# In the second cross attention, the fills of a slot's first run move in front of the turn of the running maximum

## The chip, the core and the metric

The kernel runs on one core of a Trainium2 chip. Its engines work side by side, each through its own list of instructions in order, and meet at semaphores: PE (TensorE, matmuls and transposes into the PSUM memory), DVE (VectorE), ACT (ScalarE), POOL (GpSimd) and SP, which only issues transfers. The metric is the device time of one execution in microseconds (us), as the median of several runs. The trace is one further execution, recorded instruction by instruction.

## The reference

Two decoder layers over x (4 x 512 x 256) with a context of 4 x 1601 x 256, all in fp32. Each layer is a self attention, a cross attention and a mixture of experts, each followed by a residual and a layer norm. The change touches only the cross attention of the second layer. Cut to what matters:

```
x = layernorm(context, gamma_media, beta_media)      # 1601 rows
latents = layernorm(latents, gamma_lat, beta_lat)    # 512 rows, from the layer before
kv  = concatenate((x, latents * kv_gate))            # 2113 keys
q   = latents @ Wq;  k = kv @ Wk;  v = kv @ Wv       # 8 heads of 64
sim = (q * SCALE) @ k.T                              # fp32
sim = sim - max(sim over all 2113 keys)
attn = softmax(where(valid, sim, -1e30))
out = (attn @ v) @ Wout
```

The maximum over all keys of a query is subtracted before the exponential. So no exponential of a query can be made until the scores of all its keys are there.

## The kernel before

`layer1_cross` (line 1963) cuts the work into 32 units. A unit is one of 4 batches, one of 4 pairs of heads and one half of 256 queries. Its 2113 keys lie in 17 tiles of 128, grouped into 5 runs of 4, 4, 3, 3 and 3 tiles. One step of the outer loop is called a slot here. In slot s, PE makes the scores of unit s, while DVE and ACT lower and exponentiate those of unit s-1, and PE weighs the values with the probabilities of unit s-2. Within a slot the inner loop goes over the five runs (`gi` 0 to 4). Each engine's list is written out by hand in this order; there is no scheduler.

For one slot, the names are these:

- `scores` (L2677): two matmuls a tile of keys. ACT takes the result out of PSUM and adds the mask (L2341), tile by tile; DVE keeps the running maximum over the tiles, in a PSUM bank (L2443 copies the first tile, L2445 takes the maximum with the following ones) and writes the last step into SBUF as `most`, which the trace shows as `l_w` (L2449).
- `turned` (L2688): at the head of the next slot PE transposes `most` in four matmuls, so that DVE can reduce over the partitions (`high`, L2455, gives `nm`). `turned` waits until the last tile's maximum is there.
- `spread_out` (L2695): PE spreads that maximum over a bank, after the first run's scores. DVE subtracts it from the scores from the second run on (`lower`, L2463). ACT makes the exponentials (L2318), POOL sums them (L2232 and following).
- `weigh` (L2654): PE's product of probabilities and values. In the first run it also waits for DVE to have taken the product before (`weighted`, L2471 and L2474, giving `x_o`).
- `fill`: PE makes one more input: K (keys, L2599), V (values, L2606), q (queries, L2588), N (turned context or latents, L2581), O (the output product, L2614), x and L (the next stage's routing). All share one PSUM bank, RB, one after the other. A fill waits until the fill before it has been copied away, by ACT for K, V, q, N and x.

The fills of a run are in two lists. `lead` has the first one if it is of kind q, K or V, and is made at the very head of the run. `trail` has the rest. In the first run of a slot, `trail` holds: a V fill of 4 tiles (8 matmuls) in every even slot from 2 to 30, 15 in all, behind a K fill as lead; an N fill of four transposes in slots 5, 13 and 21, behind a q fill as lead; nothing in other slots. In the slots before the first unit there is no `turned` yet.

ACT's own list for a first run is: the last exponential of unit s-2, the copies of `trail`, then the score copies. DVE's is: `high`, statistics of the next batch's context rows (L2391; at most two in the slots named above), then the running maximum over the first four tiles.

Of the kernel before, what the change touches and what calls it, by code (L numbers as in the profile page):

```python
# [1962 lines left out]
def layer1_cross(nc, top, g):  # L1963
# [20 lines left out]
    with ctx:  # L1984
# [61 lines left out]
        def unit(u):  # L2046

            return u // UB, u % UB // 2, u % 2

        def exists(u):  # L2050
            return 0 <= u < UNITS
# [6 lines left out]
        def uses(s, gi):  # L2058


            made = []
            if s == -1:
                if gi == 0:
                    for i in range(len(CGROUPS) - 1):
                        made += turns(0, i)
                    made += [("K", 0, 0, c) for c in range(PURE)] + turns(0, len(CGROUPS) - 1)
                    made += [("q", 0, 0)] + [("K", 0, 0, c) for c in range(PURE, NG)]
                return made
            b, i = s // UB, s % UB
            p = i // 2  # L2070
            if exists(s):
                if i % 2 == 0:
                    made += [("K", b, p, NG - 1)] if gi == 0 and s > 0 else []
                    made.append(("V", b, p, gi))
                else:
                    nb, np_ = (b, p + 1) if p + 1 < PAIRS_X else (b + 1, 0)
                    if nb < B:
                        made.append(("K", nb, np_, gi - 1) if gi >= 1 else ("q", nb, np_))
                if b + 1 < B and (i, gi) in TURNS:
                    made.append(("N", b + 1) + divmod(TURNS.index((i, gi)), KD))  # L2080
            if b >= 1:
                if i == 2 and gi in (2, 4):
                    made.append(("O", b - 1, gi // 2 - 1))
                if (i, gi) in ((4, 1), (4, 3)):
                    made.append(("x" if gi == 1 else "L", b - 1, 0))
                if (i, gi) in ((7, 1), (7, 3)):
                    made.append(("x" if gi == 1 else "L", b - 1, 1))
            return made

        def lead(s, gi):  # L2090

            return [use for use in uses(s, gi)[:1] if s >= 0 and use[0] in "qKV"]

        def trail(s, gi):
            return uses(s, gi)[len(lead(s, gi)):]
# [23 lines left out]
        def released(eng, use):  # L2119

            if use[0] in BY_ACT:
                eng.wait_ge(moved, MOVED[use])
            else:
                eng.wait_ge(read, READ[use])
# [10 lines left out]
        def piece_of(t):  # L2135
            return next(k for k, (lo, hi) in enumerate(PIECES) if lo <= t < hi)

        def scores_at(u, t):

            k = piece_of(t)  # L2140
            first = 2 * ((u * NPC + k) % 2)
            at = t - PIECES[k][0]
            return first, slice(at * QN, (at + 1) * QN)

        def moved_before(m):

            return m // NPC * KT + PIECES[m % NPC][1]
# [226 lines left out]
        def _(dve):  # L2374
# [10 lines left out]
            def stats(b, i):  # L2385
                src, _, np_ = source(b, i)
                if i == 0:
                    dve.wait_ge(cx_loaded, 48 * b)
                    if b >= 1:
                        dve.wait_ge(shift_ready, STATS_DONE[b - 1, 1 if b >= 2 else 0])  # L2390
                return token(nc.vector.bn_stats(bn[0:np_, i, :], src))  # L2391
# [168 lines left out]
        def _(pe):  # L2560
# [70 lines left out]
            def last_product(half, pairs):  # L2631
                for i in range(2):
                    j = 2 * half + i
                    for p in pairs:
                        mm = nc.tensor.matmul(PS[:, FINAL_OUT[half], i * D:(i + 1) * D], o[:, p, j * P:(j + 1) * P], wo[:, p, :],
                                              start=(i == 0 and p == 0), stop=(i == 1 and p == PAIRS_X - 1))
                if pairs[-1] == PAIRS_X - 1:
                    mm.then_inc(last_out, 1)

            pe.wait_ge(consts, 2)  # L2640
            for s in SLOTS:
                if s == 0:
                    pe.wait_ge(w_loaded, 16 * 3)
                for gi in range(NG):

                    def weigh(u):
                        b, p, hq = unit(u)
                        pe.wait_ge(exp_done, u * NG + gi + 1)
                        if gi == 0 and u >= 1:
                            pe.wait_ge(o_ready, u)  # L2650
                        released(pe, ("V", b, p, gi))
                        for t in TILES[gi]:
                            for h in range(2):
                                mm = nc.tensor.matmul(PS[h * HDX:(h + 1) * HDX, AVB, 0:QN],  # L2654
                                                      vs[:, p % 2, t, h * HDX:(h + 1) * HDX],
                                                      pt[:, u % 2, t, h * QN:(h + 1) * QN],
                                                      start=(t == 0), stop=False)
                        if gi == NG - 1:
                            pe.wait_ge(summed, (u + 1) * SUMS)
                            for h in range(2):  # L2660
                                mm = nc.tensor.matmul(PS[h * HDX:(h + 1) * HDX, AVB, QN:2 * QN], ones[:, 0:HDX],
                                                      total[:, h * QN:(h + 1) * QN], start=False, stop=True)
                        mm.then_inc(av_done, 1)

                    def scores():
                        b, p, hq = unit(s)
                        released(pe, ("K", b, p, gi))
                        released(pe, ("q", b, p))
                        for t in TILES[gi]:
                            k = piece_of(t)  # L2670
                            m = s * NPC + k
                            if t == PIECES[k][0] and m >= 2:
                                pe.wait_ge(s_moved, moved_before(m - 2))
                            first, half = scores_at(s, t)
                            for h in range(2):
                                at = slice(h * HDX, (h + 1) * HDX)
                                mm = nc.tensor.matmul(PS[:, first + h, half], ks[at, t * P:(t + 1) * P],  # L2677
                                                      qs[at, p % 2, hq * QN:(hq + 1) * QN], start=True, stop=True)
                            if t == PIECES[k][1] - 1:
                                mm.then_inc(s_done, 1)  # L2680

                    def turned(u):

                        pe.wait_ge(s_most, u * KT + KT)
                        if u >= 1:
                            pe.wait_ge(lowered, u * NPC)
                        for j in range(SPAN // P):
                            mm = nc.tensor.transpose(PS[:, MB, j * P:(j + 1) * P], most[:, j * P:(j + 1) * P], ident[:])  # L2688
                        mm.then_inc(t_done, 1)

                    def spread_out(u):

                        pe.wait_ge(nm_ready, u + 1)
                        for j in range(SPAN // P):
                            mm = nc.tensor.transpose(PS[:, MB, j * P:(j + 1) * P],  # L2695
                                                     nm[:, u % 2, j:j + 1].to_broadcast([P, P]), ident[:])
                        mm.then_inc(m_done, 1)

                    for use in lead(s, gi):
                        fill(use)  # L2700
                    if s == UNITS and gi == 0:
                        released(pe, BY_NUMBER[-1])
                        last_product(0, (0, 1, 2))
                        pe.wait_ge(s_moved, UNITS * KT)
                        last_product(1, (0, 1))
                    if exists(s - 2):
                        weigh(s - 2)
                    if gi == 0 and exists(s - 1):
                        turned(s - 1)
                    for use in trail(s, gi):  # L2710
                        fill(use)
                    if exists(s):
                        scores()
                    if gi == 0 and exists(s - 1):
                        spread_out(s - 1)
# [212 lines left out]
```

## Time and profile before

| what | value |
|---|---|
| median of 3 runs | 2210.22 us (2209.06 to 2211.64) |
| profiled execution | 2216.79 us, of which the span of the trace is 2214.6 us |
| PE, matmuls | 1984.1 us busy, 90% of the span |
| DVE | 1534.0 us, 69% |
| ACT | 1153.4 us, 52% |
| POOL | 963.9 us, 44% |
| second cross attention with its lead-in | about 880 to 1870 us of the span |

The page's shares are means over stages with different limits. The second cross attention is the stretch from the first score matmul at 909.9 us to the last exponential at 1849.7 us, with the opening and closing steps around it. For this change only this stretch matters, and in it the few microseconds around each `turned`, of which there are 32, one at the start of each slot from 1 to 32. From one `turned` to the next it is 26 to 36 us. In rows of the trace, matmul counts are twice those of the kernel text where the operands are fp32 products (16 for 8), while a transpose counts once.

### The profile page before, as it was taken

Reading aid. Unit: us, or ns where it says so; the run is one execution under the profiler, and the core shown is the slowest. Engines: PE = TensorE matmul, PEld = TensorE weight load, DVE = VectorE, ACT = ScalarE, POOL = GpSimd, SP = SyncE. Lnnn points to the kernel's source line nnn. Section 1 sums busy time; section 2 is a strip of 40 time slices with the busy share of each in tenths; the row PEclk is TensorE's granted clock in tenths of the full one; section 3 lists DMA queues with packets and bytes.
Section 4 is the critical chain, followed back from the end, with each engine's and each line's share of the span. In section 5 each row is a group of like instructions: output and inputs, shape, how many; then the busy total and the mean of one; then the engine's idle time right before and its main releaser. Section 6 shows DMA issues by size and latency. Waiting matters only on the chain. (4 is left out here: it accounts for less than half of the span.)

```text
span 2214.6 us, 36014 instructions
## 1 busy us (share of the span) xinstructions
PE 1984.1 (90%) x12788; PEld 1417.3 (64%) x12788; DVE 1534.0 (69%) x2463; ACT 1153.4 (52%) x2215; POOL 963.9 (44%) x752
## 2 busy tenths in 40 slices
PE   7898885997988885899999999999999996799997
PEld 4565555995654553556666666666666664699996
DVE  5677864555878988588888888888888886222223
ACT  3322311110276465677876787678876772233333
POOL 2233232222322231077666666766666675222223
PEclk9999987998899997999999999999999998899998
DMA  4100006413000000200100000000000001621113
GB/s 161 40 21 23 26 15 260 184 37 115 0 0 1 1 30 0 69 1 1 31 1 1 1 16 26 1 1 1 11 1 1 1 11 68 248 85 38 36 37 126
DMA packets 37158, 95.63 MB, mean 43 GB/s; under 512 B 5492, under 2 KB 24696, under 8 KB 32248
## 3 DMA queue, kind: packets, MB, share of 16 engines
q1 hardware_dynamic: 31032, 77.07, 9.6%
q0 software_dynamic: 5952, 16.26, 2.2%
q8 instruction: 107, 1.75, 0.3%
q14 instruction: 67, 0.55, 0.1%
HBM read 78.89 MB, written 14.42 MB: 42 GB/s over the span
## 5 line engine op out<-in xcount | busy, mean ns | idle before, releaser
L2232 POOL TENSOR_TENSOR x_total<-x_total,x_pt 128x1024 f32<-128x1024 f32 x189 | 446.7, 2363 | 152.0 <-ACT x_pt L2318 133.3
L2341 ACT ACTIVATE x_pt<-PS,x_maskf 128x512 f32<-128x512 f32 x544 | 332.6, 690 | 139.4 <-PE PS L2677 136.4
L2445 DVE TENSOR_TENSOR PS<-x_pt,PS 128x512 f32<-128x512 f32 x480 | 333.3, 694 | 48.2 <-ACT x_pt L2341 10.9
L2463 DVE TENSOR_TENSOR x_pt<-x_pt,PS 128x1024 f32<-128x1024 f32 x320 | 322.8, 1050 | 0.7 <-PE PS L2695 0.7
L2677 PE MATMUL PS<-x_qs,x_ks 64*128 64x256 f32 x2176 | 279.2, 392 | 0.0
L2318 ACT ACTIVATE x_pt<-x_pt 128x1536 f32<-128x1536 f32 (+1 forms) x160 | 264.1, 1665 | 13.4 <-DVE x_pt L2463 13.4
L2654 PE MATMUL PS<-x_pt,x_vs 128*64 128x256 f32 x2108 | 261.0, 386 | 8.3 <-issue 8.3
L1163 PEld LDWEIGHTS PS<-m_xT,m_own 128*128 128x128 f32 x1984 | 234.8, 195 | 8.3 <-DVE m_own L1243 2.9
L1163 PE MATMUL PS<-m_xT,m_own 128*128 128x128 f32 x1984 | 235.7, 278 | 4.1 <-DVE m_own L1243 2.4
L2677 PEld LDWEIGHTS PS<-x_qs,x_ks 64*128 64x128 f32 x2176 | 197.8, 187 | 61.4 <-issue 36.1
L1175 PE MATMUL PS<-f_w,m_hT 128*128 x992 | 224.0, 379 | 0.0
L2654 PEld LDWEIGHTS PS<-x_pt,x_vs 128*64 128x64 f32 x2108 | 140.3, 136 | 125.3 <-issue 66.1
L1243 DVE COPY m_own<-f_w 128x2048 f32 x62 | 76.1, 1227 | 207.4 <-PE PS L1163 184.6
L1132 POOL DMA_INDIRECT ys<-m_y,f_target x62 | 61.2, 987 | 317.6 <-DVE m_y L1258 317.6
L1175 PEld LDWEIGHTS PS<-f_w,m_hT 128*128 128x128 f32 x992 | 183.8, 190 | 22.5
L1886 PE MATMUL PS<-l_w,l_xT 128*128 128x512 f32 x384 | 178.5, 615 | 20.3 <-ACT l_qkv L1606 17.0
L1886 PEld LDWEIGHTS PS<-l_w,l_xT 128*128 128x128 f32 x384 | 72.6, 195 | 120.9 <-issue 79.0
L2232 POOL TENSOR_TENSOR x_total<-x_pt 128x1024 f32<-128x1024 f32 x32 | 75.8, 2369 | 164.2 <-ACT x_pt L2318 164.2
L1568 POOL TENSOR_TENSOR l_pp<-l_qkv 128x1024 f32<-128x1024 f32 x20 | 61.0, 3049 | 193.2 <-ACT l_qkv L1606 131.4
L2606 PE MATMUL PS<-l_w,x_kvT 128*128 128x128 f32 x1088 | 139.6, 280 | 1.6 <-DVE LG L2430 1.0
L2599 PE MATMUL PS<-x_kvT,x_wk 128*128 128x384 f32 (+1 forms) x320 | 136.4, 550 | 3.6 <-ACT x_ks L2287 2.7
L2606 PEld LDWEIGHTS PS<-l_w,x_kvT 128*128 128x128 f32 x1088 | 127.6, 192 | 18.7 <-issue 13.1
(321 smaller groups left out, 2921.7 us busy)
## 6 DMA issues: line engine op xcount, KB each, us to landing
f_w<-in_L_ffn_w SPq DMA_DIRECT2D x32, 1024.0 KB, 6.8
a_ctxT<-in_ctxT SPq DMA_DIRECT2D x8, 800.5 KB, 4.3
l_w<-in_ctx SPq DMA_DIRECT2D x4, 1024.0 KB
f_w<-ys SPq DMA_DIRECT2D x16, 256.0 KB, 5.0
l_w<-in_L_attn_w SPq DMA_DIRECT2D x6, 512.0 KB, 7.1
a_xT<-in_xT SPq DMA_DIRECT2D x4, 512.0 KB, 5.2
X<-in_x SPq DMA_DIRECT2D x1, 2048.0 KB, 10.8
xr<-a_xn SPq DMA_DIRECT2D x16, 128.0 KB, 1.7
```

The costliest lines, as they stand in the source:

```text
L1163: mm = nc.tensor.matmul(PS[:, HB + 2 * (i % 2) + c // 4, (c % 4) * P:(c % 4 + 1) * P], own[:, k * F + c * P:k * F + (c + 1) * P], xT[:, i ...
L1175: mm = nc.tensor.matmul(PS[:, YB + i % 2, 0:D], hT[:, i % 2, c, :], w2[:, bass.ds(e * (KF * D) + c * D, D)], start=(c == 0), stop=(c == KF ...
L1886: mm = nc.tensor.matmul(bank, xT[:, s, k, :], w[:, k, at], start=(k == 0), stop=(k == KD - 1))
L2232: ins = nc.gpsimd.tensor_tensor(total2[:], first, tile[:, 2 * k + 2:2 * k + 4, :], ALU.add)
L2318: nc.scalar.activation(p_, p_, ACT.Exp).then_inc(exp_done, 1)
L2341: nc.scalar.activation(pt[:, s % 2, t, :].rearrange("p (h n) -> p h n", h=2), PS[:, first:first + 2, half], ACT.Identity, bias=maskf[:, b ...
L2445: ins = nc.vector.tensor_tensor(acc, tile, acc, ALU.max)
L2463: nc.vector.tensor_tensor(p_, p_, PS[:, MB, None, :].to_broadcast([P, at.stop - at.start, SPAN]), ALU.subtract).then_inc(lowered, 1)
L2599: mm = nc.tensor.matmul(out[:, 0:at.stop - at.start], wk[:, k, p * P:(p + 1) * P], kvT[:, b % 2, k, at], start=(k == 0), stop=(k == KD - 1))
L2606: mm = nc.tensor.matmul(out[:, i * P:(i + 1) * P], kvT[:, b % 2, k, t * P:(t + 1) * P], wv[:, k, p * P:(p + 1) * P], start=(k == 0), stop= ...
L2654: mm = nc.tensor.matmul(PS[h * HDX:(h + 1) * HDX, AVB, 0:QN], vs[:, p % 2, t, h * HDX:(h + 1) * HDX], pt[:, u % 2, t, h * QN:(h + 1) * QN] ...
L2677: mm = nc.tensor.matmul(PS[:, first + h, half], ks[at, t * P:(t + 1) * P], qs[at, p % 2, hq * QN:(hq + 1) * QN], start=True, stop=True)
```

## The change

In the loop over the runs, PE's list made `turned` first and the trailing fills after it. Now it makes the trailing fills first. Nothing else differs. The lists of ACT, DVE, POOL and SP are the same, row for row, and so are PE's instructions and their number; only their order differs, at 18 places.

```diff
                     if exists(s - 2):
                         weigh(s - 2)
+                    for use in trail(s, gi):
+                        fill(use)
                     if gi == 0 and exists(s - 1):
                         turned(s - 1)
-                    for use in trail(s, gi):
-                        fill(use)
                     if exists(s):
                         scores()
                     if gi == 0 and exists(s - 1):
                         spread_out(s - 1)
```

PE's list at the head of slot 2, and likewise of the 14 other even slots up to 30. The first row is the K fill, the second `weigh`, then the V fill (L2606) and `turned` (L2688), the scores (L2677) and `spread_out` (L2695):

```order
 L2599 MATMUL PS<-x_kvT,x_wk 128x384 x2
 L2654 MATMUL PS<-x_pt,x_vs 64x256 x8
-L2688 MATMUL PS<-ident,l_w 128x128 x4
-L2606 MATMUL PS<-l_w,x_kvT 128x128 x8
+L2606 MATMUL PS<-l_w,x_kvT 128x128 x8
+L2688 MATMUL PS<-ident,l_w 128x128 x4
 L2677 MATMUL PS<-x_qs,x_ks 128x256 x8
 L2695 MATMUL PS<-ident,x_nm 128x128 x4
```

The V fill has moved past `turned`, which now stands directly in front of the scores.

PE's list at the head of slot 5, and likewise of slots 13 and 21. Here the lead is a q fill (L2588), and the fill that moves is the turn of four context tiles (L2581):

```order
 L2588 MATMUL PS<-x_latT,x_wq 128x512 x2
 L2654 MATMUL PS<-x_pt,x_vs 64x256 x8
-L2688 MATMUL PS<-ident,l_w 128x128 x4
 L2581 MATMUL PS<-ident,l_w 128x128 x4
+L2688 MATMUL PS<-ident,l_w 128x128 x4
 L2677 MATMUL PS<-x_qs,x_ks 128x256 x8
 L2695 MATMUL PS<-ident,x_nm 128x128 x4
```

The transposes of the context tiles have moved in front of those of the maximum. In the 14 slots that have no trailing fill in their first run, `turned` stood directly in front of the scores before and still does (or, in slot 32, before `spread_out`).

## Rows read from the trace of the kernel before

**Rows 1.** Busy time by engine, 1253 to 1368 us (engines, granted clock, DMA share, GB/s).

```profile
1253.00:1368.00 115.00, 113.78 (x810) 74.49 (x811) 98.08 (x135) 94.03 (x132) 74.92 (x40) 1.00 0.06 20
```

**Rows 2.** Waits in 911 to 1830 us: who <- for whom: total us, times, longest us.

```profile
DVE PS L2443 <- ACT x_pt L2341: 59.1, 30, 6.1
...
PE PS L2688 <- DVE l_w L2449: 14.6, 19, 1.9
```

**Rows 3.** Timeline of slot 8, PE (start us, us, engine, line, tiles, count, idle before <-releaser).

```profile
1123.58 1.95 PE L2654 MATMUL PS<-x_pt,x_vs 128*64 128x256 f32 x16 [0.95 <-issue]
...
1126.32 0.66 PE L2688 MATMUL PS<-ident,l_w 128*128 128x128 f32 x4 [0.79 <-DVE l_w L2449]
...
1126.81 1.95 PE L2606 MATMUL PS<-l_w,x_kvT 128*128 128x128 f32 x16
...
1128.69 2.00 PE L2677 MATMUL PS<-x_qs,x_ks 64*128 64x256 f32 x16
```

**Rows 4.** Timeline, DVE, same place.

```profile
1123.06 0.42 DVE L2474 TENSOR_TENSOR x_o<-PS,x_rb 128x256 f32<-128x256 f32 x1
...
1125.57 0.69 DVE L2449 TENSOR_TENSOR l_w<-x_pt,PS 128x512 f32<-128x512 f32 x1
...
1127.01 0.69 DVE L2455 TENSOR_REDUCE x_nm<-PS 128x4 f32<-128x512 f32 x1 [0.75 <-PE PS L2688]
...
1130.59 0.69 DVE L2443 COPY PS<-x_pt 128x512 f32<-128x512 f32 x1 [2.23 <-ACT x_pt L2341]
```

**Rows 5.** Timeline, ACT, same place.

```profile
1122.67 0.48 ACT L2287 COPY x_ks<-PS 128x384 f32<-128x384 f32 x1
...
1129.87 2.42 ACT L2341 ACTIVATE x_pt<-PS,x_maskf 128x512 f32<-128x512 f32 x4 [0.49 <-PE PS L2677]
```

**Rows 6.** Timeline of slot 9, PE, nothing between turn and scores.

```profile
1155.67 0.65 PE L2688 MATMUL PS<-ident,l_w 128*128 128x128 f32 x4 [0.79 <-DVE l_w L2449]
...
1156.25 2.00 PE L2677 MATMUL PS<-x_qs,x_ks 64*128 64x256 f32 x16
...
1158.18 0.65 PE L2695 MATMUL PS<-ident,x_nm 128*128 128x128 f32 x4
```

**Rows 7.** Timeline of slot 9, DVE, same place.

```profile
1156.36 0.69 DVE L2455 TENSOR_REDUCE x_nm<-PS 128x4 f32<-128x512 f32 x1 [0.75 <-PE PS L2688]
...
1156.97 0.74 DVE L2391 BATCH_NORM_STATS2 x_bn<-l_w 128x6 f32<-128x256 f32 x2
...
1158.15 0.69 DVE L2443 COPY PS<-x_pt 128x512 f32<-128x512 f32 x1 [0.44 <-ACT x_pt L2341]
```

**Rows 8.** Timeline of slot 6, PE, without a wait.

```profile
1066.68 1.95 PE L2654 MATMUL PS<-x_pt,x_vs 128*64 128x256 f32 x16
...
1068.59 0.66 PE L2688 MATMUL PS<-ident,l_w 128*128 128x128 f32 x4
...
1070.97 2.00 PE L2677 MATMUL PS<-x_qs,x_ks 64*128 64x256 f32 x16
```

**Rows 9.** Timeline of slot 2, PE, the longest wait.

```profile
949.68 1.95 PE L2654 MATMUL PS<-x_pt,x_vs 128*64 128x256 f32 x16
...
953.48 0.66 PE L2688 MATMUL PS<-ident,l_w 128*128 128x128 f32 x4 [1.85 <-DVE l_w L2449]
...
955.86 2.00 PE L2677 MATMUL PS<-x_qs,x_ks 64*128 64x256 f32 x16
```

**Rows 10.** Timeline, PE, the turns of slots 16 and 24.

```profile
1365.48 0.66 PE L2688 MATMUL PS<-ident,l_w 128*128 128x128 f32 x4 [0.24 <-DVE l_w L2449]
...
1604.00 0.66 PE L2688 MATMUL PS<-ident,l_w 128*128 128x128 f32 x4 [0.49 <-DVE l_w L2449]
```

**Rows 11.** Timeline of slot 5, PE, with a turn of inputs behind.

```profile
1037.17 1.95 PE L2654 MATMUL PS<-x_pt,x_vs 128*64 128x256 f32 x16
...
1039.65 0.66 PE L2688 MATMUL PS<-ident,l_w 128*128 128x128 f32 x4 [0.53 <-DVE l_w L2449]
...
1040.67 2.00 PE L2677 MATMUL PS<-x_qs,x_ks 64*128 64x256 f32 x16
```

## The prediction

> **What bounds the kernel now.** I read the busy times by stretch first, then the waits of the second cross attention, and then the timeline around each of the 32 turns of the maximum.
>
> In a typical stretch of the stage PE's matmuls are busy 113.8 of 115 us, DVE 98.1, ACT 94.0 and POOL 74.9, at a granted clock of 1.00 [rows 1]. The reader is to see two engines near their limit and not one. The Trainium skill, "Perfetto Trace Analysis", Identifying the Most-Contended Engine, would have TensorE judged by its weight loads and the other engines by their occupancy. By that DVE would be the fuller one, and a shorter wait of PE alone would bring nothing; how I weigh that stands with the first rival.
>
> Among the waits, PE stood before `turned` for DVE's last maximum 19 times, 14.6 us in all, and DVE stood before its first maximum for ACT's score copies 59.1 us in 30 slots [rows 2]. Both waits lie at the head of a slot, a few us apart.
>
> Slot 8 shows how they hang together. PE's `weigh` begins at 1123.58, right behind DVE's `x_o`, which ended at 1123.48 [rows 3, 4]. DVE then goes on without a stop to the last maximum, which ends at 1126.26. PE has been through with `weigh` since 1125.53, stands 0.79 us, makes `turned` (0.49 us to the next start), then the V fill (1.88), and only at 1128.69 the scores. ACT copies the first of them at 1129.87 [rows 5], and DVE begins its maximum at 1130.59, after 2.23 us of idleness [rows 4]. So from DVE's last work of one slot to its first of the next, everything goes through PE, and the V fill stands in that path. In the timeline of this slot DVE is at work almost without a gap from there to the next last maximum. The time of such a slot is DVE's work plus this gap, and what shortens the gap shortens the slot, for both engines.
>
> **The change part by part.** Nothing is added or removed; 18 fills swap places with `turned`. No transfer and no list of another engine moves. The V fill needs the K fill before it to have left the shared bank. In slot 8 that copy ends at 1123.15 [rows 5], long before `weigh` ends at 1125.53, so the fill can begin at once.
>
> Now the cost of a head, from the start of `weigh` to the first score matmul. `weigh` takes 1.91 us to the next start [rows 8]. I use 1.90. The V fill takes 1.88 in any slot [rows 3]. `turned` directly in front of the scores takes 0.58, as the unchanged slot 9 shows [rows 6], against 0.49 in front of a fill [rows 3]. So after the change a head without a wait is 1.90 + 1.88 + 0.58 = 4.36 us.
>
> Slot 8 has 1128.69 - 1123.58 = 5.11 us now. `turned` would be free to start at 1123.58 + 3.78 = 1127.36, over a microsecond after DVE's maximum, so its wait is gone. The gain is 5.11 - 4.36 = 0.75 us. Nine of the 15 even slots show the same wait of 0.79 us (2 lies apart, below), and they give 9 x 0.75 = 6.75.
>
> Slot 2 waits 1.85 us, and its head is 955.86 - 949.68 = 6.18 [rows 9]. DVE's maximum is there at about 953.42. The fill ends at 953.46 by the same sum, so the wait is just covered: a gain of 6.18 - 4.38 = 1.80.
>
> Slots 16 and 24 wait 0.24 and 0.49 [rows 10]. By the difference seen in slot 8, gain = wait less 0.04, they give 0.20 and 0.45.
>
> Slots 6, 14 and 22 don't wait. Slot 6 has 1070.97 - 1066.68 = 4.29 now [rows 8], and would have 4.36; taking 0.09 for `turned`'s dearer place, they lose 3 x 0.09 = 0.27.
>
> Slot 5 waits 0.53, and its fill of four transposes takes 1040.67 - 1039.65 - 0.49 = 0.53 [rows 11]. It fits the wait. The scores could then start at 1039.65 + 0.58 = 1040.23, a gain of 0.44. Slots 13 and 21 have no wait and lose 2 x 0.09 = 0.18.
>
> The sum: 6.75 + 1.80 + 0.20 + 0.45 + 0.44 - 0.27 - 0.18 = 9.2 us.
>
> **What is late next, and who waits longer.** `turned` itself comes later: in slot 8 at 1127.36 instead of 1126.32. Behind it on DVE stand the reduction (L2455), up to two statistics, and the first maximum. Unchanged slots already have this shape. In slot 9 the reduction starts 0.69 us after `turned`, takes 0.69, two statistics take 0.74, and DVE still stands 0.44 us for ACT [rows 6, 7]. So DVE's branch is hidden behind the scores' branch, by 0.44 us where there are two statistics. The changed slots have two or none. `spread_out` starts 2.51 us after `turned` in slot 9 [rows 6] and finds the reduction done. If that cover were gone, each further 0.1 us on DVE's branch beyond the 0.44 would cost 0.1 us a slot.
>
> The copy of V on ACT lies before the score copies in ACT's list. It comes at about 1127.4 instead of 1128.8, when ACT has nothing else, since it stood idle for PE there.
>
> What the trace doesn't show is PE passing from `weigh` into a V fill, and from a V fill into `turned`. The next rows are `weigh` into `turned`, 1.91 [rows 8], and V into the scores, 1.88 [rows 3]. Below, such a passage could save the 0.09 that `turned` costs more, over 18 heads 1.6 us. Above, I allow 0.17 us each for two passages, double the 0.09 seen between the two kinds of neighbour: 0.34 x 18 = 6.1 us. I take nothing, nearest to the rows, and keep -1.6 and +6.1.
>
> A rule bears on this wait. The row first: V's matmuls take 1.88 us when `turned` has stood before them for a semaphore [rows 3], just as in a full stream. The Trainium skill, "TensorE: Matmul & The Clock Gate", Step-by-step, says that PE may pull weight loads ahead of matmuls in flight but keeps the matmuls in order. By that a wait on `turned` holds back everything behind it but at most a weight load, so the fill behind didn't profit from the wait already, and the sum stays at 9.2; had it profited by one load, the sum would be smaller by part of a matmul a slot.
>
> **The rivals.**
>
> *The wait comes back.* DVE, not PE, sets the pace in the nine slots with 0.79; the microsecond won at the head returns as a longer wait of PE for `x_o` or for the last maximum. Then these nine give nothing, and the rest gives 9.2 - 6.75 = 2.4 us. For it speaks that both waits of PE are for DVE, and that DVE is 85% busy [rows 1]; it is what the rule on contended engines amounts to. Against it, DVE itself stands 2.23 us in this very gap, for scores that lie behind the fill [rows 4]. Time by the runs: 2210.2 - 2.4 = 2207.8.
>
> *The new neighbours cost.* Each of the 18 heads pays the 0.34 above: 9.2 - 6.1 = 3.1 us gained, 2207.1. For it speaks only that the passage into the scores differs by 0.09 with the neighbour; against it, that all others agree within 0.03.
>
> *Slower: the maximum comes too late.* DVE's queue is held at its head until `turned` is done. If reduction, statistics and first maximum were then the longer branch, the delay of `turned` would pass into each slot. In slot 8 it is 1127.36 - 1126.32 = 1.04 us; by 18 that is 18.7, less the 9.2: 9.5 us slower, 2219.7. It decides from the point where DVE's branch outlasts the scores' branch, that is at over 0.44 us more than in slot 9. Slot 9 is the evidence against it [rows 7].
>
> *It doesn't do what it says*: if the V fill waited for ACT's copy of K in most slots, `turned` would be held up too. The copy ended 2.4 us early in slot 8 [rows 5]; I count this with the slower case.
>
> **How the numbers follow.** Against the profiled execution, 2216.79 us, the forecast is 2216.79 - 9.2 = 2207.6. That execution lay 6.6 us above the median of the runs, 2210.22, all of it outside what the change touches. For the median it is 2210.2 - 9.2 = 2201.0.
>
> Chances: the forecast 0.79, with its own range of 2199 to 2204 (the low end from the 1.6 us, the high end from slots whose waits are only partly won). The wait comes back 0.10. New neighbours 0.07. Slower 0.04. The 80% range reaches from 2198, below the own range for the scatter of the runs, to 2208, which takes in the two cases of a small gain. A measurement of this kernel can tell some 0.2%, 4.4 us, from no change. The forecast is faster by 0.4%; the two middle cases lie within 0.2%. So faster 0.79, same 0.17, slower 0.04.
>
> **What would show it.** In the changed kernel the waits of PE before `turned` should fall from 14.6 us to some 4.4, in the six unchanged odd slots alone. DVE's wait before the reduction grows, by 1.04 us in slots like 8, while its wait before the first maximum, 59.1 us, should fall to about half: in a slot like 8 by 1.04 + 0.75 = 1.8 us. From `weigh` to scores each changed V head should read about 4.36 us. The stage should be 9 us shorter and the rest equal. The prediction is wrong if PE's idle time before `weigh`, which ends with DVE's `x_o`, grows by as much as the other falls, if DVE's first maximum starts without waiting in the changed slots, or if heads read 4.6 us and more.

## The result and the profile after

The changed kernel is faster. In the first timing its median was 2199.64 us (2198.01 to 2200.31, 5 runs) beside 2209.1 us for the kernel before (2208.88 to 2211.64, 5 runs); the ratio is 0.9943, with a 95% interval of 0.9929 to 0.9958. The bare quotient of the two medians is 0.9957, near the upper end of that interval. The forecast was 2201.0 us against 2210.2, a ratio of 0.9958. Two further timings of the same kernel, told below, gave 0.9960 (0.9946 to 0.9973) and 0.9955 (0.9942 to 0.9969).

The profiled execution took 2199.34 us, with a span of 2197.3 us. DVE, ACT and POOL are busy as long as before within 1.4 us. PE's matmul time reads 1976.6 us against 1984.1, but 1985.4 and 1984.8 in two later traces of the same kernel (e4 and e9), so that difference is scatter. Nothing became cheaper; it is waiting that went. The waits of the cross attention, up to the last slots (engine, line, whom it waited for: us in total, times, longest us):

```profile
DVE x_nm L2455 <- PE PS L2688: 44.3, 31, 2.6
...
DVE PS L2443 <- ACT x_pt L2341: 31.3, 30, 6.5
...
PE PS L2688 <- DVE l_w L2449: 5.4, 7, 1.0
```

These answer to [rows 2], and the first of them to this row of the kernel before:

```profile
DVE x_nm L2455 <- PE PS L2688: 26.4, 31, 1.5
```

PE's wait before the turn fell from 14.6 us in 19 slots to 5.4 in 7. DVE's wait before its first maximum fell from 59.1 to 31.3 us, and its wait for the turn itself rose from 26.4 to 44.3. The head of slot 8, all engines (start us, us, engine, line, operation, tiles, count, idle before):

```profile
1111.52 0.42 DVE L2474 TENSOR_TENSOR x_o<-PS,x_rb 128x256 f32<-128x256 f32 x1
...
1112.04 1.95 PE L2654 MATMUL PS<-x_pt,x_vs 128*64 128x256 f32 x16 [0.95 <-issue]
...
1113.92 2.05 PE L2606 MATMUL PS<-l_w,x_kvT 128*128 128x128 f32 x16
1114.03 0.69 DVE L2449 TENSOR_TENSOR l_w<-x_pt,PS 128x512 f32<-128x512 f32 x1
...
1115.81 0.60 PE L2688 MATMUL PS<-ident,l_w 128*128 128x128 f32 x4
1116.01 0.58 ACT L2290 COPY x_vs<-PS 128x512 f32<-128x512 f32 x1 [1.64 <-PE PS L2606]
...
1116.34 2.00 PE L2677 MATMUL PS<-x_qs,x_ks 64*128 64x256 f32 x16
1116.45 0.69 DVE L2455 TENSOR_REDUCE x_nm<-PS 128x4 f32<-128x512 f32 x1 [1.72 <-PE PS L2688]
...
1118.24 0.69 DVE L2443 COPY PS<-x_pt 128x512 f32<-128x512 f32 x1 [0.44 <-ACT x_pt L2341]
...
1118.27 0.65 PE L2695 MATMUL PS<-ident,x_nm 128*128 128x128 f32 x4
```

They answer to [rows 3 to 5]. The V fill (L2606) starts 1.88 us after `weigh`, while DVE is still at its last maximum, which ends at 1114.72. `turned` starts at 1115.81, without a wait, and the scores 0.53 us later. From `weigh` to scores it is 4.30 us, where it was 5.11. The reduction (L2455) waits 1.72 us now, and the first maximum waits 0.44, as it already did in slot 9 [rows 7].

Slot 6, where PE had not waited before:

```profile
1055.14 1.95 PE L2654 MATMUL PS<-x_pt,x_vs 128*64 128x256 f32 x16
...
1057.01 1.86 PEld L2606 LDWEIGHTS PS<-l_w,x_kvT 128*128 128x128 f32 x16 [0.38 <-issue]
...
1058.90 0.60 PE L2688 MATMUL PS<-ident,l_w 128*128 128x128 f32 x4
...
1059.43 2.00 PE L2677 MATMUL PS<-x_qs,x_ks 64*128 64x256 f32 x16
...
1061.33 0.69 DVE L2443 COPY PS<-x_pt 128x512 f32<-128x512 f32 x1 [1.10 <-ACT x_pt L2341]
```

It takes 1059.43 - 1055.14 = 4.29 us, within 0.01 us of before [rows 8], and DVE's first maximum still waits 1.10 us. The later turn cost nothing here.

All heads together, from the timelines of the two traces. The table gives the time from the start of `weigh` to the first score matmul, and for slot 2 what the slot gained in all:

| slots | before, us | after, us | gain of each | forecast of each |
|---|---|---|---|---|
| 4, 8, 10, 12, 18, 20, 26, 28, 30 | 5.11 | 4.30 | 0.81 | 0.75 |
| 2 | 6.17 | 5.53 (`weigh` began 1.1 earlier) | 1.8 | 1.80 |
| 16 | 4.56 | 4.30 | 0.26 | 0.20 |
| 24 | 4.81 | 4.30 | 0.52 | 0.45 |
| 5 | 3.50 | 3.07 | 0.43 | 0.44 |
| 6, 14, 22 | 4.28 | 4.30 | -0.01 | -0.09 |
| 13, 21 | 2.90 | 2.90 | 0 | -0.09 |

From the turn of slot 1 to that of slot 32 it was 907.98 us before and is 897.73 now: 10.25 us less, and the gains of the table add up to 10.3. That is the measure of the stage used below. By it the ratio should be 1 - 10.25 / 2210 = 0.9954.

### The profile page after: what moved, and what is told of

Read it like the earlier page. It is cut to its first block and busy times, and to the rows that moved or that the text cites. A ratio compares the mean times of both kernels' runs of the same rounds, so it can differ in the third digit from the quotient of the medians.

```text
span 2197.3 us, 36014 instructions
## 1 busy us (share of the span) xinstructions
PE 1976.6 (90%) x12788; PEld 1414.9 (64%) x12788; DVE 1534.2 (70%) x2463; ACT 1152.0 (52%) x2215; POOL 964.8 (44%) x752
## 5 line engine op out<-in xcount | busy, mean ns | idle before, releaser
L2677 PE MATMUL PS<-x_qs,x_ks 64*128 64x256 f32 x2176 | 278.2, 392 | 0.0
L2677 PEld LDWEIGHTS PS<-x_qs,x_ks 64*128 64x128 f32 x2176 | 197.3, 186 | 61.1 <-issue 38.1
L2606 PEld LDWEIGHTS PS<-l_w,x_kvT 128*128 128x128 f32 x1088 | 127.5, 192 | 24.4 <-issue 18.9
L2606 PE MATMUL PS<-l_w,x_kvT 128*128 128x128 f32 x1088 | 141.2, 281 | 1.6 <-DVE LG L2430 1.0
```

The costliest lines, as they stand in the source:

```text
L2606: mm = nc.tensor.matmul(out[:, i * P:(i + 1) * P], kvT[:, b % 2, k, t * P:(t + 1) * P], wv[:, k, p * P:(p + 1) * P], start=(k == 0), stop= ...
```

## The experiments

There are ten experiments, three of them without an edit (e1, e4, e9). The measure of the stage, beside the ratio to the kernel before:

| kernel | stage, us | against before | ratio (95% interval) |
|---|---|---|---|
| before | 907.98 | | |
| the changed kernel, first time | 897.73 | -10.3 | 0.9943 (0.9929 to 0.9958) |
| e1, the same again | 907.96 | 0.0 | 1.0000 (0.9991 to 1.0010) |
| e2, swap where PE didn't wait | 907.98 | 0.0 | 1.0001 (0.9992 to 1.0010) |
| e3, swap in the nine slots | 900.60 | -7.4 | 0.9971 (0.9959 to 0.9982) |
| e4, the changed kernel again | 897.72 | -10.3 | 0.9960 (0.9946 to 0.9973) |
| e9, the changed kernel, third time | 897.64 | -10.3 | 0.9955 (0.9942 to 0.9969) |
| e5, turn behind the scores | 926.49 | +18.5 | 1.0106 (1.0088 to 1.0123) |
| e6, V fill behind the scores | 915.80 | +7.8 | 1.0048 (1.0035 to 1.0060) |
| e7, V fill in front of `weigh` | 898.95 | -9.0 | 0.9962 (0.9949 to 0.9974) |
| e8, scores in front of the turn, five slots | 893.33 | -14.7 | 0.9937 (0.9924 to 0.9949) |
| e10, the same in six slots | see below | | 0.9929 (0.9915 to 0.9942) |

**e1: the kernel before, unchanged.** It has no edit.

> The kernel before once more, unchanged, for the scatter between executions and for a second trace. The first trace of before was 2216.79 us, 6.6 above its median, and 8.5 us of its distance to the changed kernel's trace lie ahead of slot 1. If that is scatter of one execution, this trace starts slot 1 at another place (within 10 us of 927.6), the granted clock of the stretch in slot 1 that read 0.83 reads about 1.00 here, and all 32 heads read as before within 0.02 us: the stage from slot 1's scores to slot 32's turn as long as before, less about 1.1. Rival: the stretch ahead is shorter only in the changed kernel; then this trace starts slot 1 at 927 to 928. Ratio 1.000 within 0.002.

Measured: the profiled execution took 2210.59 us. Slot 1's turn was at 920.87, not at 927.59, and all heads read as before within 0.02 us. So the 6.7 us by which the trace of before began its stage later belongs to that one execution. The eleven traces besides the first one of before, of all kernels, put this turn from 919.1 to 925.4. The other 1.1 us did not behave as expected. A slow stretch stands in slot 1 of this trace too. The first row is from the trace of before, the two others from about the same place in two traces of the changed kernel (its first, and that of e4); columns are the time window, its length, busy time of PE, its weight loads, DVE, ACT and POOL, then the granted clock:

```profile
940.00:950.00 10.00, 7.82 (x36) 4.43 (x38) 9.58 (x16) 7.86 (x12) 6.73 (x4) 0.83 0.00 0
```

```profile
931.00:941.00 10.00, 7.38 (x44) 4.21 (x44) 9.58 (x20) 8.78 (x13) 6.71 (x4) 1.00 0.00 0
```

```profile
940.00:950.00 10.00, 8.61 (x41) 4.91 (x42) 9.48 (x17) 9.06 (x13) 8.50 (x6) 0.83 0.01 2
```

The granted clock was 0.83, 1.00 and 0.83: a part of the stretch at the lower level of 1.2 GHz in two of the three, each right after PE had stood 2.2 us for ACT's copy of K. The trace at 1.00 had stood just as long. Of the twelve traces ten show the lower clock there and two do not (the changed kernel's first and e10's). But the stage is 897.73 us at 1.00 and 897.72 at 0.83. In slot 1 DVE's last maximum ends last either way, so what PE loses there comes off its wait before the next turn: 1.02 us at 1.00, none at 0.83. I had taken 1.1 us off the gain for it, in the expectations of e1 and e4; that was wrong.

**e2: the swap only where PE had not waited.**

```diff
+                    early = s in (6, 13, 14, 21, 22)
+                    if early: fill the trailing ones
                     if gi == 0 and exists(s - 1):
                         turned(s - 1)
-                    for use in trail(s, gi):
+                    if not early: fill the trailing ones
```

> Swap only in the five slots where PE did not wait (6, 13, 14, 21, 22). Prediction's step: each loses 0.09, 0.45 us in all. Against it, from the changed kernel's trace, where such heads read 4.29 and 2.90 as before: nothing at all, 0.0 us. Rival that the late maximum costs: DVE's wait before its first maximum in slots 6, 14, 22, 2.89 us before, would fall to zero and the head-to-head time grow; I expect it to fall to about 1.0 and no time to be lost. Ratio 1.000 within 0.001.

Measured: the same stage within 0.03 us. In slot 6, DVE:

```profile
1059.65 0.69 DVE L2449 TENSOR_TENSOR l_w<-x_pt,PS 128x512 f32<-128x512 f32 x1
1062.89 0.69 DVE L2455 TENSOR_REDUCE x_nm<-PS 128x4 f32<-128x512 f32 x1 [2.55 <-PE PS L2688]
1064.69 0.69 DVE L2443 COPY PS<-x_pt 128x512 f32<-128x512 f32 x1 [1.10 <-ACT x_pt L2341]
```

DVE waits 2.55 us for the turn and still 1.10 us for the first score. Its branch is not the longer one. The prediction's loss of 0.09 a slot isn't there: the heads of slots 6, 14 and 22 grew by 0.01 us, those of 13 and 21 by nothing.

**e3: the swap only in the nine slots with a wait of 0.79 us.** The edit is as in e2, with the slots 4, 8, 10, 12, 18, 20, 26, 28 and 30.

> Swap only in the nine slots with a wait of 0.79 us (4, 8, 10, 12, 18, 20, 26, 28, 30). Gap theory: 9 x 0.81 = 7.3 us less, ratio 0.9967. Rival that the wait comes back (DVE sets the pace): 0 us, and PE's idle time before weigh grows from 0.3 to 1.0 us by about 0.8 in these slots or those behind them. Waits of PE before the turn: 14.6 - 7.1 = 7.5 us.

Measured: 907.98 - 900.60 = 7.38 us, 0.82 a slot. The waits:

```profile
PE PS L2654 <- issue: 8.3, 10, 1.7
...
PE PS L2688 <- DVE l_w L2449: 7.5, 10, 1.9
```

PE's wait before the turn is 7.5 us, as expected. Its wait before `weigh`, where the time would have had to come back, is 8.3 us by the same count of 10 waits as in the kernel before (8.30 from slot 1 to 32). In the changed kernel itself it is 8.3 us too. The rival that the wait comes back is excluded.

**e4 and e9: the changed kernel twice more.** No edit; each was timed beside the kernel before.

> The changed kernel again, timed with the others, for a narrower interval. By its trace the stage gained 10.25 us from slot 1's scores on, of which 1.1 are a slow stretch in the trace of before: 9.1. Theory: ratio 0.9958. Rival from the first timing (ratio 0.9943): 12.6 us, so that 3 us more were gained somewhere outside the stage; then this ratio is again below 0.995.

> The changed kernel a third time. The first timing gave a ratio of 0.9943, the second 0.9960; the stage is 10.25 us shorter in both traces, which is 0.9954. If that is all, this ratio lies at 0.9954 within its interval, and the mean of the three within 0.001 of it. If something outside the stage is gained too, it lies at 0.9943 again.

Measured: the stage is 897.72 and 897.64 us, the ratios 0.9960 and 0.9955 (as bare quotients of medians 0.9964 and 0.9959). The mean of the three ratios is 0.9953, that of the three quotients 0.9960, and the stage alone gives 0.9954. No gain outside the stage shows, as far as timings can tell; the first ratio lay low within its interval.

**e5: the turn one step later still.**

```diff
                     for use in trail(s, gi):
                         fill(use)
-                    if gi == 0 and exists(s - 1):
-                        turned(s - 1)
                     if exists(s):
                         scores()
+                    if gi == 0 and exists(s - 1):
+                        turned(s - 1)
```

> The changed kernel with the turn of the maximum moved one step further back, behind the first run's scores, in all 32 slots; DVE's list as it is, so DVE stands at the head of its queue until the turn is done. This drives the slower rival past its point. From unchanged heads: the turn would start 1.93 us after the scores start, the reduction 0.69 later and take 0.69, statistics 0.74 where there are two, so DVE's first maximum starts 3.4 to 4.1 us after the scores start and not 1.9; spread_out on PE waits for the reduction about 0.9 us. Less the 0.53 to 0.58 by which the scores come earlier: 0.9 us a slot, 20 to 35 us slower than the changed kernel, ratio to before 1.005 to 1.011. If instead a late maximum were harmless at any distance, the time would be that of the changed kernel or 10 us less. DVE's wait before its first maximum, 31 us, falls to nearly zero.

Measured: 28.8 us longer in the stage than the changed kernel, ratio 1.0106. Slot 1's own turn comes later here, so the distance of the turns leaves a little out: from the first score matmul to the turn of slot 32 it is 945.26 us, 29.9 more than the 915.41 of the changed kernel. Slot 32 has no scores, and nothing moves there. Slot 9, where the trace shows the branch that is now the longer one:

```profile
1151.71 2.00 PE L2677 MATMUL PS<-x_qs,x_ks 64*128 64x256 f32 x16
1151.82 0.69 DVE L2449 TENSOR_TENSOR l_w<-x_pt,PS 128x512 f32<-128x512 f32 x1
...
1153.63 0.42 PEld L2688 LDWEIGHTS PS<-ident,l_w 128*128 128x128 f32 x4 [0.33 <-issue]
...
1154.33 0.69 DVE L2455 TENSOR_REDUCE x_nm<-PS 128x4 f32<-128x512 f32 x1 [1.82 <-PE PS L2688]
1154.94 0.74 DVE L2391 BATCH_NORM_STATS2 x_bn<-l_w 128x6 f32<-128x256 f32 x2
...
1155.08 0.65 PE L2695 MATMUL PS<-ident,x_nm 128*128 128x128 f32 x4 [0.78 <-DVE x_nm L2455]
...
1155.60 0.68 DVE L2443 COPY PS<-x_pt 128x512 f32<-128x512 f32 x1
```

The scores start at 1151.71, at once behind `weigh`. But DVE stands 1.82 us for the turn at the head of its queue, and its first maximum starts 3.89 us after the scores, where it was 1.91 in the changed kernel. PE waits 0.78 us before `spread_out`, for the reduction. So the mechanism of the slower rival is real; in the actual change it stays 0.44 us and more from its point.

**e6: the V fill out of the head, behind the scores.**

```diff
                     if gi == 0 and exists(s - 1):
                         turned(s - 1)
-                    for use in trail(s, gi):
-                        fill(use)
                     if exists(s):
                         scores()
                     if gi == 0 and exists(s - 1):
                         spread_out(s - 1)
+                    if late: fill the trailing ones      # even slots, first run
```

In these slots `weigh` of the second run goes in front of its V fill, and ACT's copy of V behind the score copies.

> The kernel before with the V fill of the 15 even slots moved the other way: out of the head, behind the scores and spread_out, the next run's weigh between it and the next V fill; ACT's copy of it behind the score copies. Two theories. If only DVE's gap counts (from its last maximum to its first), it falls from 4.33 to 2.54 us, more than in the changed kernel (3.52), and the time falls further: nine tied slots x 1.8, 16 us below before, ratio 0.993. If PE's own idle time is what was won, the 0.79 before the turn stays in all nine, and only where PE stands idle later in the same slot is there anything to win: slots 8, 16 and 30 with 1.1, 1.1 and 1.8, slots 2, 4 and 24 with 0.6 each, 5.8 us in all, ratio 0.9974, which is 4.5 us slower than the changed kernel. I hold the second the likelier. Waits before the turn stay at about 10 us or more.

Measured: neither. The stage is 7.8 us longer than before. First slot 8:

```profile
1123.10 1.60 PEld L2682 LDWEIGHTS PS<-x_qs,x_ks 64*128 64x128 f32 x16 [0.17 <-issue]
...
1125.00 0.69 DVE L2448 COPY PS<-x_pt 128x512 f32<-128x512 f32 x1 [0.44 <-ACT x_pt L2343]
...
1125.51 1.95 PE L2611 MATMUL PS<-l_w,x_kvT 128*128 128x128 f32 x16
...
1127.39 1.49 PEld L2659 LDWEIGHTS PS<-x_pt,x_vs 128*64 128x64 f32 x16
...
1129.27 1.86 PEld L2611 LDWEIGHTS PS<-l_w,x_kvT 128*128 128x128 f32 x16 [0.39 <-issue]
...
1131.25 1.60 PEld L2682 LDWEIGHTS PS<-x_qs,x_ks 64*128 64x128 f32 x16
...
1133.16 1.50 DVE L2450 TENSOR_TENSOR PS<-x_pt,PS 128x512 f32<-128x512 f32 x2 [1.67 <-ACT x_pt L2343]
```

DVE's first maximum now starts early, as the first theory had it, 2.54 us after its last. But between the first run's scores and the second's there stand two V fills and a `weigh`, 1123.10 to 1131.25, 8.15 us instead of 6.17, and DVE runs dry there: 1.67 us before L2450. What it won at the head it lost behind: from the turn of slot 8 to that of slot 9 it is 29.34 us, where it was 29.35. Over the stage DVE's waits before its first maximum fell from 59.1 to 32.8 us, and those before L2450 rose to 43.2, against 10.9 before. PE's wait of 0.79 us before the turn stays in all nine slots, as the second theory had it, but the gain that it named elsewhere did not come: slots 4, 8, 16, 24 and 30 are as long as before within 0.03 us. Both theories had missed the gap behind the first run.

So the moved fill explains why nothing was won, and not the 7.8 us. These lie in other slots, by the distances between turns: 0.94 us in each of slots 6, 12, 14, 20, 22 and 28, 0.2 in 10, 18 and 26, and 1.6 in slot 2. In the six, another fill follows in the second run, and the edit has moved away the `weigh` that stood between it and the V fill. PE now stands 0.68 us before it for ACT's copy of V. Slot 14:

```profile
1311.27 2.05 PE L2611 MATMUL PS<-l_w,x_kvT 128*128 128x128 f32 x16
...
1313.36 0.59 ACT L2290 COPY x_vs<-PS 128x512 f32<-128x512 f32 x1 [2.77 <-PE PS L2611]
...
1313.99 0.28 PE L2586 MATMUL PS<-ident,l_w 65*128 65x65 f32 x1 [0.68 <-ACT x_vs L2290]
```

In slot 2 the granted clock was 0.83 over 946 to 956 us, a part of it at the lower level, and the scores and `spread_out` took 3.30 and 0.99 us instead of 2.00 and 0.65:

```profile
947.72 3.30 PE L2682 MATMUL PS<-x_qs,x_ks 64*128 64x256 f32 x16
950.95 0.99 PE L2700 MATMUL PS<-ident,x_nm 128*128 128x128 f32 x4
```

**e7: the V fill in front of `weigh` too, in six slots.** The edit is the changed kernel with `fill` of the trailing use ahead of `weigh` in the first run of slots 4, 8, 10, 12, 18 and 20.

> The changed kernel, and in the six slots where PE also waits for DVE before weigh (4, 8, 10, 12, 18, 20; 0.5 to 0.97 us each) the V fill goes in front of weigh. It needs ACT's copy of K, which in slot 8 ends 0.43 us before weigh may start. So it can use some 0.4 us of the wait: 6 x 0.35 = 2 us less than the changed kernel, stage from 897.7 to 895.7, ratio to before 0.9945. Rival: the copy of K is too late and weigh starts later by as much as the fill takes, so that nothing is won or up to 1.88 us a slot is lost.

Measured: 1.2 us longer in the stage than the changed kernel; the rival. Slot 12:

```profile
1230.83 0.60 ACT L2311 ACTIVATE l_w<-l_w,x_shift,x_rs 128x256 f32<-128x256 f32 x1
1231.32 0.60 ACT L2356 ACTIVATE X<-X,x_shift,x_rs 128x256 f32<-128x256 f32 x1
...
1231.81 0.48 ACT L2287 COPY x_ks<-PS 128x384 f32<-128x384 f32 x1
...
1232.34 2.05 PE L2606 MATMUL PS<-l_w,x_kvT 128*128 128x128 f32 x16 [1.37 <-ACT x_ks L2287]
...
1234.32 1.95 PE L2654 MATMUL PS<-x_pt,x_vs 128*64 128x256 f32 x16
```

In slot 8 the wait for ACT's copy of K was 0.57 us, as foreseen, and the slot gained 0.2. In slots 12 and 20 ACT has two normalisations in front of that copy (L2311, L2356), PE waits 1.37 us for it, and each of the two slots loses 0.6. In slot 18 PE waits 0.57 us where it had stood only 0.51 before `weigh`, and the slot loses 0.2. I had taken one slot's order for that of six.

**e8: the scores in front of the turn, in the five odd slots that still wait.**

```diff
 # PE, slots 3, 9, 17, 25, 31
-                        turned(s - 1)
                         scores()
-                        spread_out(s - 1)
+                        turned(s - 1)
 # PE, second run, behind the leading fill
+                        spread_out(s - 1)
 # DVE, first run
-                        high(s - 1)
                         for t in TILES[gi]:
                             highest(s, t)
+                            if t == 1: high(s - 1)
```

> The changed kernel, and in the five odd slots where PE still waits 0.64 to 0.79 us before the turn (3, 9, 17, 25, 31) the scores go in front of the turn, DVE makes the reduction behind its second tile's maximum, and spread_out goes behind the next run's fill. DVE's gap then falls from 2.54 to about 1.12 us, and its reduction of 0.69 goes into its stream: 0.7 us a slot, 5 x 0.7 = 3.5 us less than the changed kernel, stage from 897.7 to 894.2, ratio to before 0.994. Rival: the reduction and spread_out come too late for the lowering, DVE waits for them, and the 0.7 turns into a loss of the same size.

Measured: 4.4 us shorter in the stage than the changed kernel, 0.9 a slot, a little more than expected. Slot 9:

```profile
1142.88 1.95 PE L2657 MATMUL PS<-x_pt,x_vs 128*64 128x256 f32 x16 [0.30 <-issue]
...
1144.76 1.60 PEld L2680 LDWEIGHTS PS<-x_qs,x_ks 64*128 64x128 f32 x16 [0.39 <-issue]
...
1144.87 0.69 DVE L2450 TENSOR_TENSOR l_w<-x_pt,PS 128x512 f32<-128x512 f32 x1
...
1146.66 0.69 DVE L2444 COPY PS<-x_pt 128x512 f32<-128x512 f32 x1 [0.44 <-ACT x_pt L2342]
1146.69 0.42 PEld L2691 LDWEIGHTS PS<-ident,l_w 128*128 128x128 f32 x4 [0.33 <-issue]
...
1148.07 0.69 DVE L2456 TENSOR_REDUCE x_nm<-PS 128x4 f32<-128x512 f32 x1
...
1148.90 0.60 PE L2698 MATMUL PS<-ident,x_nm 128*128 128x128 f32 x4
...
1150.06 1.22 DVE L2464 TENSOR_TENSOR x_pt<-x_pt,PS 128x1024 f32<-128x1024 f32 x1
```

This is e5's order of scores and turn on PE, in five slots, with `spread_out` one step later still and DVE's list changed to fit it. The first maximum starts at 1146.66, 1.10 us after the last one's end at 1145.56, the reduction finds the turn done, and `spread_out` doesn't wait. Only in slot 31, where no fill follows, does it wait, 1.46 us; that slot gained 0.7. In e5, with DVE's list as it was, 29 of the 31 distances between turns were longer than in the changed kernel. How much of the difference is DVE's list and how much the later `spread_out` was not tried apart.

**e10: and in slot 1.**

> As the kernel with the scores in front of the turn in five odd slots, and in slot 1 too, where PE waits 0.77 us. That kernel's stage was 4.4 us shorter than the changed kernel's, 0.9 us a slot. Here another 0.5 to 0.9 us, stage 893.3 to 892.6 by the distance of the turns of slots 1 and 32, but the turn of slot 1 itself comes 1.3 us later against its scores, so that the distance alone would read 891.2; ratio 0.993. Rival: slot 1 has three statistics in front of the first maximum, DVE gains nothing, and the time is that of the five-slot kernel.

Measured: ratio 0.9929, median 2194.91 us beside 2210.01. From the first score matmul of all to the turn of slot 32 it is 909.84 us; e8 has 911.01, the changed kernel 915.41, before 925.66. The sixth slot gave 1.2 us, more than expected. By the distance of the turns this kernel reads 891.07, close to the 891.2 foreseen. It is the fastest of all, and beats the changed kernel by about 0.25%.

## Why the prediction was right or wrong

The direction, the mechanism and the place were right, and the size nearly so: 9.2 us forecast, 10.25 measured in the stage, 10.4 by the mean of three ratios (0.0047 x 2210), 8.9 by the medians alone. Yet the range did not do its work. The first ratio, 0.9943, put on the median that the range was made for, is 2210.2 x 0.9943 = 2197.6 us, 0.4 below its low end of 2198. The median of the runs, 2199.64, lies inside. Of the 3.4 us between 2201.0 and 2197.6, 1.05 are the stage's, and belong to the step named next. The other 2.3 are not in the stage, and neither later timing has them: scatter of one timing, for which the range had no room.

- *The gap from DVE's last maximum to its first goes through PE, and the V fill stands in it.* Right. e3 shows it in isolation, at 0.82 us a slot. In e6 the fill was out of this gap and stood in the next one, and slot 8 was as long as before: where no wait of PE is covered, nothing is won.
- *A head without a wait is 4.36 us.* Too large by 0.06; it measured 4.30. This is the step that failed, a term too dear and not a wrong mechanism. `turned` in front of the scores takes 0.53 us behind a V fill that leaves it no wait, where I had set the 0.58 that it takes behind `weigh` in slot 9 [rows 6]; and `weigh` takes 1.88 into the V fill, where I had set 1.90. The nine slots gave 0.81 and not 0.75, together 0.5 us more.
- *Slots without a wait lose 0.09 each.* The same term again. They lose 0.01 us at most, as e2 shows; 0.4 us more. A V fill and a turn cost the same in either order within that, and so do two sets of transposes. Slots 16 and 24 gave 0.13 us more for the same reason. Together some 1.05 us, which is the distance between 9.2 and 10.25.
- *Slot 2 gains 1.80, slot 5 0.44.* Right within 0.02.
- *The low end of the range.* It let the new neighbours save 1.6 us at most, which covers the 1.05, and allowed next to nothing for the scatter of a timing. Five runs against five told the ratio only within 0.15%, or 3.3 us. The low end should have been some 3 us below the forecast's own, at 2196 to 2197.
- *The wait comes back* (0.10): excluded by e3. *The new neighbours cost* (0.07): they do not; a head is 0.06 us shorter than forecast. *The maximum comes too late* (0.04): not reached; e5 shows its price, 28.8 us with the turn behind the scores in slots 1 to 31.
- *DVE is the fuller engine, so a shorter wait of PE brings nothing.* The Trainium skill, "Perfetto Trace Analysis", Identifying the Most-Contended Engine, read by occupancy alone, would have said so. The trace sides with its next section, Optimization Strategy, which asks what blocks the gaps on that engine: 1.79 of DVE's gap of 2.23 us went when PE's V fill moved.
- *What would show it*: of the waits of PE before the turn 4.4 us in six odd slots are left in e4 and e9, as forecast; the first trace has 1.02 more in slot 2. DVE's wait before the first maximum fell by 1.79 us in slot 8 (1.8 forecast), and its wait before the reduction grew by 0.97 (1.04 forecast). PE's wait before `weigh`, which was to grow if the prediction was wrong, stayed at 8.3 us.

## What to carry to other kernels

An instruction that waits at the head of an in-order queue is best preceded by work that does not depend on it, as far as that work can start without a wait of its own; count what stands between two engines' turns, not each engine's busy share. Before a fill, a copy or a product is moved, look at every place where it would go, one by one: the same move won 0.2 us in slot 8 and lost 0.6 in slot 12 (e7), and in e6 most of the loss came where a `weigh` between two fills had been moved away. A slot that shows the intended effect is not yet the slot in which the time was lost. And where the waited-for step is itself short, try the pair of lists together. Scores in front of the turn cost 28.8 us in all slots with DVE's list unchanged (e5), and gained 4.4 us in the five slots that still waited, with DVE's list and `spread_out` adapted (e8).

## What the runs showed of the hardware

- Four fp32 transposes directly in front of the scores took 0.58 us to the next start behind `weigh`, with or without a wait (slots 9 and 7 of the kernel before). Behind a fill they took 0.53 where they had not waited, and 0.58 where they had: slot 2 of the changed kernel waits 1.02 us, and in slot 5 `turned` starts 0.06 us after DVE's last maximum ends, as it does in slot 9 after a listed wait, so it waited there too, too briefly to be listed. The figures repeat within 0.01 us from slot to slot. Why is not known.
- From one execution to the next the stage repeats within 0.1 us (897.64 to 897.73 in three traces of the changed kernel, 907.96 and 907.98 in two of the kernel before), while the stretch ahead of it varied by over 8 us. The distance of two marks in a trace tells a change of 0.1 us; the timings told 3.
- The granted clock was 0.83 over 10 us in slot 1 in ten of twelve traces and 1.00 in two with about the same wait of 2.2 us before it, and the stage took as long either way, since PE waited for DVE behind it. In e6 it was 0.83 in slot 2 as well, and there the slot took 1.6 us longer.
